# First attention of a fused transformer kernel: diagonal blocks without their masked quarter, blocks dealt out anew, value projection in one block

## The reference

```python
q, k, v = (einsum('bnd,fd->bnf', x, W).reshape(b, n, 16, 64).transpose(0, 2, 1, 3) for W in (Wq, Wk, Wv))
sim = einsum('bhid,bhjd->bhij', q, k) * 64 ** -0.5
sim = 50.0 * tanh(sim / 50.0)
sim = where(tril(ones((n, n))), sim, finfo.min)
attn = softmax(sim, axis=-1)
out = einsum('bhij,bhjd->bhid', attn, v)       # then the heads side by side, times Wo
```

## Time and profile before

| | |
|---|---|
| Median of 3 runs | 1215.64 us (1214.12 to 1220.51) |
| Profiled execution | 1214.02 us, span 1212.3 us |
| TensorE busy | 1127.0 us, 93% of the span |
| VectorE busy | 862.3 us, 71% |
| ScalarE busy | 705.0 us, 58% |
| GpSimd busy | 522.3 us, 43% |
| First attention | from 55.77 us (first scores) to about 427 us |

### The profile page before, as it was taken

How to read it: one execution, slowest core, us unless ns; L and a number is a source line. 1 busy time by engine, 2 the same in 40 slices (tenths; PEclk the granted TensorE clock), 3 DMA queues, 4 the chain that set the end, 5 groups by cost and what they waited for, 6 DMA issues and landing times. The chain is left out here.

```text
span 1212.3 us, 29054 instructions
## 1 busy us (share of the span) xinstructions
PE 1127.0 (93%) x10981; PEld 628.2 (52%) x10981; DVE 862.3 (71%) x1805; ACT 705.0 (58%) x915; POOL 522.3 (43%) x529
## 2 busy tenths in 40 slices
PE   3799999999999998889997999999999999788998
PEld 1356566566665775469973222222222222547996
DVE  6466778778778465854426899999999992585442
ACT  4687877777778434512226277777777778451221
POOL 0066567667566400358843123322421331035884
PEclk9999999999999997979999999999999999797999
DMA  4001010010010102237742112221122110224665
GB/s 129 1 9 27 21 42 24 18 42 24 18 42 20 39 18 84 95 93 194 182 93 85 51 44 63 64 54 54 58 60 59 51 47 18 96 82 117 183 172 125
DMA packets 60345, 81.83 MB, mean 67 GB/s; under 512 B 23488, under 2 KB 41284, under 8 KB 59612
## 3 DMA queue, kind: packets, MB, share of 16 engines
q1 hardware_dynamic: 48180, 70.54, 19.3%
q0 software_dynamic: 10880, 8.86, 4.9%
q10 hardware_dynamic: 1192, 1.19, 0.3%
HBM read 55.12 MB, written 15.72 MB: 58 GB/s over the span
## 5 line engine op out<-in xcount | busy, mean ns | idle before, releaser
L2020 ACT ACTIVATE at_PR<-psum 128x1024 f32<-128x1024 f32 x256 | 248.1, 1021 | 107.2 <-PE psum L2267 105.2
L2089 DVE TENSOR_REDUCE at_MX<-psum 128x1 f32<-128x512 f32 x468 | 298.4, 684 | 11.7 <-PE psum L2239 8.9
L511 ACT ACTIVATE PR<-psum 128x1024 f32<-128x1024 f32 x144 | 146.3, 1021 | 72.2 <-PE psum L841 61.4
L860 PE MATMUL psum<-PR,V 64*64 64x256 f32 (+1 forms) x2560 | 172.0, 357 | 4.0 <-issue 1.5
L841 PE MATMUL psum<-Q,K 64*64 64x512 f32 (+2 forms) x1792 | 151.8, 437 | 2.1 <-ACT PR L511 2.1
L860 PEld LDWEIGHTS psum<-PR,V 64*64 64x64 f32 x2560 | 96.3, 133 | 98.9 <-issue 88.8
L516 ACT ACTIVATE PR<-PR 128x1024 f32<-128x1024 f32 x144 | 143.7, 1050 | 0.0
L2284 PE MATMUL psum<-at_PR,at_VG 128*32 128x512 f32 x1024 | 136.2, 604 | 0.8 <-POOL at_PR L1957 0.8
L1957 POOL TENSOR_TENSOR at_PR<-at_PR,at_FAC 128x512 f32<-128x512 f32 x64 | 81.1, 1267 | 101.7 <-ACT at_PR L2020 101.7
L1549 PE MATMUL psum<-moe_XGT,moe_WE 128*128 128x256 f32 x512 | 124.7, 388 | 0.2
L488 POOL TENSOR_SCALAR_AFFINE_SELECT PR<-PR 128x256 f32<-128x256 f32 (+1 forms) x80 | 54.2, 682 | 155.1 <-ACT PR L516 154.8
(11 more groups left out here) (267 smaller groups left out, 1858.9 us busy)
## 6 DMA issues: line engine op xcount, KB each, us to landing
moe_WE<-in_c_We SPq DMA_DIRECT2D x32, 768.0 KB, 4.6
XB<-at_r_dram SPq DMA_DIRECT2D x32, 256.0 KB, 3.8
at_outs_dram<-at_OTS SPq DMA_DIRECT2D x15, 256.0 KB, 2.9
moe_rows_dram<-XNS SPq DMA_DIRECT2D x2, 1152.0 KB, 12.0
moe_spare_dram<-moe_zeros SPq DMA_DIRECT2D x2, 1024.0 KB, 14.6
moe_sum_dram<-XB SPq DMA_DIRECT2D x2, 1024.0 KB, 3.8
moe_SG<-moe_spare_dram SPq DMA_DIRECT2D x8, 256.0 KB
at_KU<-in_c_max_krows SPq DMA_DIRECT2D x16, 128.0 KB
```

Source lines behind the costliest of these rows:

```text
L511: act.activation(PR[u][:, :, :], S[(b + u) % 2][:, :, :], ACT.Tanh, scale=SCALE0 / CLAMP).then_inc(z.clamped, 1)
L860: mm = pe.matmul(O[row[h], q:q + w], V[rows, b, j, row[h]], PR[u][rows, h, at:at + w], start=(first and u == 0), stop=(not first and u == ...
L2020: act.activation(PR[:, gu % PRS, 2 * r:2 * r + 2, :].rearrange("p h n -> p (h n)"), g.psum[:, 2 * r * BANK:(2 * r + 2) * BANK], ACT.Exp).t ...
L2089: dve.tensor_reduce(MX[:, c // 32 % 2, 8 * (c % 2) + 4 * pair + I % 4, khalf:khalf + 1], bank(("max", c))[:, :], AX, ALU.max).then_inc(z.r ...
```

## The change

- **Skipped quarters.** In a diagonal block with keys 64 to 127 and queries 0 to 63 everything is masked. `scores` and `multiply` leave these 64 columns out (`hidden`). For this the key halves of blocks j = 0, 1, 6, 7 (`SWAPPED`) are exchanged in the array, by `keys(j, c)` and `half(j, c)`.
- **Units dealt out anew.** `BLOCKS` and `ADDS` are new. Diagonal blocks stood in units 0, 3, 5, 6 and 8 (unit 5 diagonal blocks alone); now they stand in 4, 7 and 8 (unit 8 alone). Unit 0 has nothing to add; unit 1 has an add of 512 columns. `READ_LAST` says which adds a clamp has to wait for. For units of several pieces the pieces are taken alternately from the near and the far two blocks.
- **Masks.** A diagonal unit gets two instructions, each on its own blocks: a select for blocks in plain order, and a TENSOR_TENSOR product with a triangle `TRI` of ones and zeros for swapped ones. `TRI` is made by three GpSimd instructions at the start.
- **Value projection.** `project_values` contracts all 128 channels at once in 128x64 tiles and stands as one block behind n = 4 and n = 13; behind n = 3 and 12 nothing stands now.

```diff
-BLOCKS = [[(0, 2), (0, 3), (0, 0), (0, 1)], [(0, 4), (0, 5), (0, 6), (0, 7)], [(1, 2), (1, 3), (1, 6), (1, 7)],
-          [(2, 2), (2, 3), (2, 6), (2, 7)], [(3, 4), (3, 5), (3, 6), (3, 7)], [(3, 3), (5, 5), (1, 1), (7, 7)],
-          [(4, 4), (4, 5), (4, 6), (4, 7)], [(1, 4), (1, 5), (5, 6), (5, 7)], [(2, 4), (2, 5), (6, 6), (6, 7)]]
+BLOCKS = [[(0, 2), (0, 3), (0, 6), (0, 7)], [(1, 2), (1, 3), (1, 6), (1, 7)], [(2, 4), (2, 5), (2, 6), (2, 7)],
+          [(3, 4), (3, 5), (3, 6), (3, 7)], [(2, 2), (2, 3), (0, 0), (0, 1)], [(0, 4), (0, 5), (4, 6), (4, 7)],
+          [(1, 4), (1, 5), (5, 6), (5, 7)], [(4, 4), (4, 5), (6, 6), (6, 7)], [(3, 3), (5, 5), (1, 1), (7, 7)]]
+SWAPPED = (0, 1, 6, 7)
+ALL_DIAGONAL = len(BLOCKS) - 1
...
-ADDS = [[(256, slice(2, 3), (0, slice(1, 2)), None)],
-        [],
-        [(256, slice(0, 1), (0, slice(0, 1)), (2, slice(0, 1))), (256, slice(3, 4), (1, slice(1, 2)), (2, slice(1, 2)))],
-        [(256, slice(0, 4, 3), None, (3, slice(0, 2)))],
-        [(256, slice(1, 2), (1, slice(0, 1)), (4, slice(0, 1))), (256, slice(3, 4), None, (4, slice(1, 2)))],
-        [(128, slice(1, 8, 2), None, (5, slice(0, 4)))],
+ADDS = [[],
+        [(256, slice(0, 4, 3), (0, slice(0, 2)), (1, slice(0, 2)))],
+        [(256, slice(3, 4), None, (2, slice(1, 2)))],
+        [(256, slice(1, 2), (2, slice(0, 1)), (3, slice(0, 1))), (256, slice(3, 4), None, (3, slice(1, 2)))],
+        [(256, slice(2, 3), (4, slice(1, 2)), None), (256, slice(0, 1), None, (4, slice(0, 1)))],
+        [(256, slice(1, 4, 2), None, (5, slice(0, 2)))],
         [(256, slice(1, 4, 2), None, (6, slice(0, 2)))],
         [(256, slice(1, 4, 2), None, (7, slice(0, 2)))],
-        [(256, slice(1, 4, 2), None, (8, slice(0, 2)))]]
+        [(128, slice(1, 4, 2), None, (8, slice(0, 4, 2))), (128, slice(5, 8, 2), None, (8, slice(1, 4, 2)))]]
+READ_LAST = [1, 1, 3, 3, 4, 5, 6, 7, 8]
...
+        def half(j, c):
+            return 1 - c if j in SWAPPED else c
+        def keys(j, c):
+            return j * P + DH0 * half(j, c)
+        def hidden(j, q, c):
+            return DH0 if half(j, c) == 1 and q == ORDER.index(j) * P else 0
...
-                    last = pool.affine_select(out=blocks, in_=blocks, compare_op=ALU.is_ge, fill=0.0, base=0,
-                                              pattern=[[0, 8 if whole else 2], [1, P]], channel_multiplier=-1)
-                    last.then_inc(z.masked, 1)
+                    plain, turned = (v[:, 0::2, :], v[:, 1::2, :]) if u == ALL_DIAGONAL else (v[:, 0::4, :], v[:, 2::4, :])
+                    count = plain.shape[1]
+                    pool.affine_select(out=plain, in_=plain, compare_op=ALU.is_ge, fill=0.0, base=0,
+                                       pattern=[[0, count], [1, P]], channel_multiplier=-1).then_inc(z.masked, 1)
+                    pool.tensor_tensor(turned, turned, bcast(TRI[:, :].unsqueeze(1), [P, count, P]), ALU.mult
+                                       ).then_inc(z.masked, 1)
...
+                def project_values(s, b):
+                    pe.wait_ge(z.key, 2 * s + 2)
+                    passed(s)
+                    for x in range(2):
+                        for t in range(4):
+                            for c in range(2):
+                                at = b * SEQ + keys(4 * x + t, c)
+                                mm = pe.matmul(J[x][row[c], t * P:(t + 1) * P], g.XT[:, at:at + DH0], W[:, 2, :],
+                                               start=True, stop=True, skip_group_check=True)
+                        mm.then_inc(z.projected, 1)
...
-                    for j, at, q, w in (near if joined else near + far):
+                    for j, at, q, w in (near if joined else [piece for pieces in zip(near, far) for piece in pieces]):
                         for h in range(2):
                             for c in range(2):
-                                into, of = S[(b + u) % 2][row[c], h, at:at + w], Q[row[h], b, q:q + w]
+                                skip = hidden(j, q, c)
+                                into, of = S[(b + u) % 2][row[c], h, at + skip:at + w], Q[row[h], b, q + skip:q + w]
...
-                                    mm = pe.matmul(O[row[h], q:q + w], V[rows, b, j, row[h]], PR[u][rows, h, at:at + w],
+                                    mm = pe.matmul(O[row[h], q + skip:q + w], V[row[part], b, j, row[h]],
+                                                   PR[u][row[part], h, at + skip:at + w],
...
-                        if 1 <= k <= 4 and (n < NU or more):
-                            project(2 * p + 1 + n // NU, 1 - n // NU, (k + 1) // 2, k % 2 == 1)
+                        if 1 <= k <= 2 and (n < NU or more):
+                            project(2 * p + 1 + n // NU, 1 - n // NU, 1, k == 1)
+                        if k == 4 and (n < NU or more):
+                            project_values(2 * p + 1 + n // NU, 1 - n // NU)
```

More of the change, by code:

```diff
@@ L500, in _ @@
                 pool.memset(g.ones[:, :], 1.0).then_inc(z.ones, 1)
+                pool.memset(TRI[:, :], 1.0).then_inc(z.triangle, 1)
+                pool.wait_ge(z.triangle, 1)
+                pool.affine_select(out=TRI[row[0], :], in_=TRI[row[0], :], compare_op=ALU.is_ge, fill=0.0, base=-DH0,
+                                   pattern=[[1, P]], channel_multiplier=-1).then_inc(z.triangle, 1)
+                pool.wait_ge(z.triangle, 2)
+                pool.affine_select(out=TRI[row[1], 0:DH0], in_=TRI[row[1], 0:DH0], compare_op=ALU.is_ge, fill=0.0, base=0,
+                                   pattern=[[1, DH0]], channel_multiplier=-1).then_inc(z.triangle, 1)
+                pool.wait_ge(z.triangle, 3)
                 span(pair)(pool)
@@ L804, in project @@
                     elif first:
-                        pe.wait_ge((z.query, z.key)[side - 1], 2 * s + 2)
-                    if not first:
-                        pe.wait_ge(z.part_projected, 3 * s + side - 2)
+                        pe.wait_ge(z.query, 2 * s + 2)
+                    else:
+                        pe.wait_ge(z.part_projected, 2 * s + side - 1)
                     passed(s)
-                    for t in range(4 if side == 2 else 1):
-                        for x in range(2):
-                            rows = row[x if first else 1 - x]
-                            for c in range(2):
-                                if side < 2:
-                                    mm = pe.matmul(J[x][row[c], :], W[rows, side, row[c]], project_from(side, b, x, rows),
-                                                   start=first, stop=not first, skip_group_check=True)
-                                else:
-                                    at = b * SEQ + x * BANK + t * P + DH0 * c
-                                    mm = pe.matmul(J[x][row[c], t * P:(t + 1) * P], g.XT[rows, at:at + DH0], W[rows, 2, :],
-                                                   start=first and t == 0, stop=not first, skip_group_check=True)
-                            if not first and (side < 2 or t == 3):
-                                mm.then_inc(z.projected, 1)
@@ L822, in project @@
+                    for x in range(2):
+                        rows = row[x if first else 1 - x]
+                        for c in range(2):
+                            mm = pe.matmul(J[x][row[c], :], W[rows, side, row[c]], project_from(side, b, x, rows),
+                                           start=first, stop=not first, skip_group_check=True)
+                        if not first:
+                            mm.then_inc(z.projected, 1)
                     if first:
                         mm.then_inc(z.part_projected, 1)
+                def project_values(s, b):
+                    pe.wait_ge(z.key, 2 * s + 2)
+                    passed(s)
+                    for x in range(2):
+                        for t in range(4):
+                            for c in range(2):
+                                at = b * SEQ + keys(4 * x + t, c)
+                                mm = pe.matmul(J[x][row[c], t * P:(t + 1) * P], g.XT[:, at:at + DH0], W[:, 2, :],
+                                               start=True, stop=True, skip_group_check=True)
+                        mm.then_inc(z.projected, 1)
@@ L840, in scores @@
                                     of = split(Q[row[h], b, :], 2 * P)[:, q // (2 * P)::(far[0][2] - q) // (2 * P), :]
-                                mm = pe.matmul(into, K[row[h], b, j * P + DH0 * c:j * P + DH0 * (c + 1)], of,
+                                mm = pe.matmul(into, K[row[h], b, keys(j, c):keys(j, c) + DH0], of,
                                                start=True, stop=True, skip_group_check=True)
@@ L856, in multiply @@
                         for side in range(2):
[L857 removed]
+                            part = side if first != swap else 1 - side
                             for j, at, q, w in PIECES[u][side][n:n + 1]:
+                                skip = hidden(j, q, part)
```

(2 more changed lines are left out.)

25 lines of the change are left out of this document (13 added, 12 removed).

## The result

The changed kernel takes 1221.53 us (median of 20 runs, 1219.17 to 1228.03), the one before 1217.23 (20 runs), ratio 1.0044, 95% interval 1.0034 to 1.0055. Run again in another series it took 1219.26 us against 1216.66, ratio 1.0035 [1.0017, 1.0054]. So it is 3 to 4 us slower; 1220 was forecast. Of the runs further down, one of the kernel e_pad2 (1823.28 us at a mean granted clock of 0.57) stands in no median. The profiled execution takes 1223.3 us, its span is 1221.5.

What follows compares the result with a forecast made beforehand. TensorE's matmul widths were taken as the bound, except at totals and handovers of O. Terms -9.5+8.4+4.5+1.1 = +4.5 us on 1214.0 gave 1218.5 profiled, 1220 us median; range 1210 to 1228, likeliest case 1216 to 1224.

Steps and rivals of the forecast that it cites:

- Columns saved: Scores and products of units 4, 7 and 8 on TensorE: skipped columns save 13.7 us, of which 9.5 us remain.
- (A): Rival: in scores of units 7 and 8 a group costs its widest record; 4.8 us slower, 1225 us; chance 0.17.
- (D): Rival: groups 64 columns wide cost more than half of 128; at no gain 4.7 us, 1225 us; chance 0.10.
- The new wait: Handover to n=9: VectorE adds unit 1, released by exp 10, before taking O; 1.05 us, 8 times, +8.4 us.
- (B): Rival: unit 1's add doesn't hold the take of O before n=9; 10.1 us less, 1210 us; chance 0.15.
- Value block: Value projection in 128x64 tiles: equal work, but change of tiling costs 0.30 us, 15 times, +4.5 us.
- Masks: GpSimd's selects and triangle products, about 4.9 us a sequence: cost nothing; without the cover 0.5 us x 8.
- Handover at n = 0: Unit 1's add at n=1 fills VectorE's 0.95 us idle and costs nothing; if it doesn't fit, up to 0.5 us x 7.
- (C): Rival: VectorE is late at n=1 too, 7 x 0.5 us, 1223.5 us; chance 0.13.
- Tail: End of the last pair: products 16 wait for exp 16 and its masks, starting near 407.0; +1.1 us.

Runs made afterwards that it cites:

- e_pad2: The changed kernel with two further always-met waits in each of TensorE's 64 calls of a pair: 1221.31 us (nine runs), ratio 1.0042 to the kernel before.

## Why the prediction was right in sum, and wrong in two of its terms

1220.0 was forecast, +4.5 us; measured are +4.3 and +2.6. But that is two errors with opposite signs, which cancel by luck: the wait was put 6.5 us too high, the tail 3 to 5 too low, and the rest lies in smaller terms and in the first and the last pair.

- **Columns saved, -9.5.** Right, and by the reasons given. The widths count quadrant by quadrant (0.76, 0.67, 0.23 us), so (A) and (D) are out. The Trainium skill's rule of strict order in start and end ("TensorE: Matmul & The Clock Gate", Part 3) would have put the scores of unit 7 at 0.86 (an estimate from the widths); the trace has 0.76, and it stays so in another order of the pieces. With nothing skipped a pair takes 1.65 us longer: 1.29 of the columns, as worked out, and the rest the late take at n = 0. The skips also hold VectorE's margin there, 0.22 us in the changed kernel; the text had it at 0.5.
- **The new wait, +8.4.** The mechanism is right: 4.39 us with the add released by exp 10 in front of the take, and 3.71 once the take goes first. The size is wrong: 0.24 us over the kernel before and not 1.05, so some 2 us instead of 8.4. The step that failed is "the add 1.27 with GpSimd adding beside it": the group's mean of rows 5 mixes adds in which VectorE was first with such in which it was second. Here it starts 0.04 us ahead of GpSimd's and takes 0.69 (row at 218.77), one of the bounds named, and from the take's start to products 9 it is 1.38, not 1.64. Link by link the chain from the end of scores 11 is 0.40 to clamp 11, 0.92 to exp 10, 1.08 to the add, 0.61 to the take and 1.38 to products 9, 4.39 us; forecast were 0.26, 0.92, 1.20, 1.19 and 1.64, 5.21. Why the last link is shorter isn't shown. (B) is out: the add does hold the take. Taking it away brings 5 us, half of the 10.1 that (B) put.
- **Value block, +4.5.** The trace shows 0.34 us lost a visit, forecast 0.30. Undoing it for one batch brought 0.22, as 0.14 goes into the wait for unit 8's masks; undoing it for both cost 15 us, by pauses that the prediction did not have at all and that come together with fetched code. As a price of the change the term stands, as a proposal to undo it would have misled.
- **Masks, nothing.** Right in the middle pairs, though with less to spare than thought: the cover is the value block itself. In the last pair TensorE waits 0.48 us for unit 8's masks.
- **Handover at n = 0, nothing.** Right: 2.03 us before and after, and (C) did not happen.
- **Tail, +1.1.** Wrong: +6.3 and +4.0 us between the last take and the last matmul of the output projection. The step that failed is "0.2 and masks of 1.3 make its products start near 407.0": it puts the masks right behind exp 16. GpSimd's queue had three adds of n = 13 to 15 in front of them, 4.94 us (row at 405.69), and masks for unit 16 (u = 7) that TensorE needs at once are new there; before, only unit 17's masks stood in that slot. From the last take to products 16 it is 15.55 us in the first profile and 14.77 in the second, before 11.84: 3.7 and 2.9 us more. Then comes what the text did not cost at all: behind the pause the clock is at 1.2 GHz, for 6.8 us in the first profile and 3.4 in the second, and from products 16 to the last matmul it is 2.6 and 1.1 us longer than before. The 0.8 us between the two up to products 16 go with the fall of the clock in front of n = 13 that only the first one has. Masks ahead of the adds give back 1.5 us, a filled pause 3 more; with both the tail is as short as before (48.9 and 49.3 us), so these two causes leave nothing over beyond the scatter of the tail (53.3 to 55.6 us).

Added up by what was measured: wait 8 x 0.24 = 1.9, value block 15 x 0.34 = 5.1, columns -9.5 make -2.5 us; between takes the first pair is 0.5 and the last 0.9 us longer than the middle ones and the kernel before account for (masks, and n = 9 of the last pair), which leaves -1.1, as measured from the first scores to the last take. With the tail's +4 to +6 that is +3 to +5.

Open is whether the pauses of the kernel with both calls split come from the loop's length at all: 1622 and 1626 instructions a pair run with one packet in 220 us, 1682 to 1690 with 18, but the only kernel above 1626 is also the only one with the second batch's call split. The short pauses stand in front of a value call of that half. Open too is where the edge would lie. The Trainium skill, "Advanced Engine Details and Errata", ISA Cache, gives TensorE 128 KB in lines of 16 KB or 256 instructions. The size of the packets agrees (16 KB). By its figures 2,048 instructions would fit (an estimate), and here a loop of 1,690 recorded ones already fetches.

## What to carry to other kernels

When an add, a copy or a mask gets a new place in an engine's order, look for everything queued in front of it and behind it up to the end of the loop's last pass, where the cover is thinnest: here the wait costs 2 us over all pairs and the tail 4 to 6, and moving the take by one unit (5 us in the profile) was worth more than all saved columns net of their costs. A shape's mean duration isn't a price: look up the single rows with the same neighbour on the other engine. And when a block is split into more instructions, look at the queue that carries instructions: here packets in the middle of the loop came with pauses that no semaphore explains.

## What the runs showed of the hardware

- A loop on TensorE with 1626 recorded instructions a pass fetches one packet between 160 and 380 us; one with 1682 to 1690 fetches 18 of them, of 16 KB, all in every second pass, and TensorE stands still four times in these passes, for 3.26, 1.04, 3.37 and 1.04 us. That the length is the cause is not shown.
- Adds of 128x512 on VectorE and GpSimd that run side by side are unequal, and which one starts first matters. VectorE first by 0.04 us: VectorE 0.69, GpSimd 1.78. GpSimd first by 0.25 us: GpSimd 1.45, VectorE 1.76. With VectorE first by 0.62 us, but an add of 256 columns still running on GpSimd (after, 195.46), it is 1.22 and 1.73.
- The 64-wide groups of a 64x64 quadrant cost half of the 128-wide (0.23 us for 16 records), and unequal widths in the four quadrants don't wait for each other.
- Going from 64x64 to 128x64 tiles costs 0.14 us in front, 0.05 behind, and 0.15 in the block itself (1.90 us for 1.75 of width).
- The granted clock falls to 0.50 behind pauses of 3.0 to 4.8 us of TensorE in the last pair and comes back 3.4 to 6.8 us later; with the pause filled it stays at 1.00. A pause's length doesn't settle it: behind 1.96 us it fell in one execution and behind 1.97 not in another of the same kernel, and behind 3.26 it fell and behind 3.37 not in one execution.
- A wait that is always met, one in each call, leaves no trace at all; a second one in the same call costs about 5 ns each (0.30 us for 64).
